# Linear attention on one Trainium2 core: one block for rows, convolution, projection and residual in place of two

## The chip, the cores and the metric

The kernel runs on one core of a Trainium2 chip. It is one program: two decoder layers over 2048 rows of 256 features, float32 outside, with a cross attention to 1601 context rows in each layer. The metric is the device time of the whole program in microseconds. The engines are TensorE (PE, with PEld for its weight loads), VectorE (DVE), ScalarE (ACT), GpSimd (POOL) and SyncE (SP); each works through its own queue in order, and they wait for one another through semaphores.

## What the part in question computes

The second layer's self attention is a linear attention with a short convolution over rows. Cut to what matters:

```python
q = _norm_last(_norm_last(jax.nn.relu(q) + EPS) ** 3)      # k the same
kv = jnp.einsum('bhnd,bhne->bhde', k, v)
z = 1.0 / (jnp.einsum('bhnd,bhd->bhn', q, k.sum(axis=2)) + EPS)
out = jnp.einsum('bhnd,bhde,bhn->bhne', q, kv, z)
xp = jnp.pad(out, ((0, 0), (1, 1), (0, 0)))
conv = xp[:, 0:N] * w_dwc[:, 0] + xp[:, 1:N + 1] * w_dwc[:, 1] + xp[:, 2:N + 2] * w_dwc[:, 2] + b_dwc
x = x + (out + conv) @ w_proj.T + b_proj
```

Each row of `out + conv` needs the row before and the row behind it, so a tile of 128 rows needs one row of each neighbour tile.

## The kernel before

There are T = 16 tiles of 128 rows. `focused_qkv` leaves the normalised q rows in `qf` (the profile calls the tensor q_rows) and the accumulated k-by-v product in the PSUM tensor `ps_kv`. Then the stage in question has two blocks with a barrier of all engines between them.

**Block one, `linear_attention`.** VectorE first builds `bd`, the block-diagonal k-by-v matrix with 8 more columns for the denominators. Then per tile n, with two buffers of each kind: GpSimd copies the q rows to `qs` (L1505); TensorE transposes them (`turn_q`, L1514); ScalarE evicts them to `qt` (`turned`, L1558); TensorE multiplies by `bd` into `ps_n` (L1530); VectorE adds the epsilon to the denominators (L1595), takes the reciprocal (L1597) and scales the numerators into `o` (L1600); TensorE transposes `o` (`turn_o`, L1521); ScalarE evicts it to `ot`, which has features on partitions and rows on the free axis (L1551), and evicts it two more times, once per half of the features, into `yt` with the middle tap and the tap bias (L1553). After the last tile VectorE adds the left and the right tap for all 2048 rows in four instructions of 2048 elements per partition (L1610).

**Block two, `linear`, called with `direct`.** ScalarE copies a tile of `yt` to `xt` (L221), TensorE projects it with four matmul records per tile (L199), VectorE adds the product to `x` (L297) and takes the row statistics with bn_stats (L299). Beside it GpSimd adds the projection's bias to `x` (L306). VectorE's add waits for that.

Behind both comes `layer_norm()`, which needs the statistics of all tiles, and then `one_head_setup`. Names in the profile: lqs, lqt, lpsq, lpsn, lpso, lo, lz, lrz, lot are the tensors of block one, conv_out is `yt`, x_res is `x`, stats is `st`.

## Time and profile before

| what | us |
|---|---|
| time, median of 3 runs (range) | 1981.6 (1980.54 to 1982.35) |
| time of the profiled execution | 1982.44 |
| its span | 1980.7 |
| VectorE's first instruction of block one starts | 1630.61 |
| VectorE's last bn_stats of block two ends (1688.97 + 0.43) | 1689.40 |

The span is the time between the first and the last recorded instruction; the profiled execution took 1.74 us more than its span. The two last lines are times from the start of the span. A timeline row has the start, the duration, the engine, the line of the kernel, the operation with output and inputs, how many instructions were merged into it, and in brackets how long the engine had been idle and who released it.

### The profile page before, as it was taken

How to read it: one execution, taken by the hardware profiler on the slowest of the kernel's cores; microseconds unless marked ns; L12 is line 12 of the kernel's file. 1: busy time of each engine (PE TensorE's matmuls, PEld its weight loads, DVE VectorE, ACT ScalarE, POOL GpSimd, SP SyncE). 2: the span in 40 equal slices, each digit the busy share in tenths (PEclk: the TensorE clock that was granted, in tenths of full speed). 3: DMA queues.
4: the chain of work that ended last, by engine and by line, in shares of the span. 5: the costliest groups of instructions: out<-in, count | busy, mean ns of one | idle time of the engine just before them, and what ended most of it. 6: DMA issues, size and time to landing. Idle time of an engine off the chain costs nothing. (4 is left out here: it accounts for less than half of the span.)

```text
span 1980.7 us, 39829 instructions
## 1 busy us (share of the span) xinstructions
PE 1725.5 (87%) x15104; PEld 694.0 (35%) x15104; DVE 1611.1 (81%) x2278; ACT 1357.1 (69%) x2607; POOL 334.5 (17%) x605
## 2 busy tenths in 40 slices
PE   7757989999999999998999999999889766499972
PEld 3421222332332233233222222222444344266651
DVE  3789999989989998887999999996578686666647
ACT  3324979889889988987999999999533445244432
POOL 0810001111121111002101010100245233000004
PEclk9966999999999999999999999999999898799995
DMA  4000000000000000100000000000300000000001
GB/s 125 0 0 1 2 1 1 2 1 1 2 1 2 1 1 1 52 1 1 2 1 2 2 1 2 1 1 2 110 1 1 1 0 1 0 1 1 1 2 42
DMA packets 12687, 18.59 MB, mean 9 GB/s; under 512 B 1856, under 2 KB 10560, under 8 KB 12256
## 3 DMA queue, kind: packets, MB, share of 16 engines
q1 hardware_dynamic: 11664, 14.78, 2.3%
q8 instruction: 121, 1.98, 0.4%
q10 hardware_dynamic: 848, 1.38, 0.2%
q14 instruction: 54, 0.44, 0.1%
HBM read 14.07 MB, written 2.10 MB: 8 GB/s over the span
## 5 line engine op out<-in xcount | busy, mean ns | idle before, releaser
L985 DVE TENSOR_REDUCE mxp<-ps_m 128x2 f32<-128x1024 f32 (+1 forms) x960 | 1088.6, 1187 | 93.7 <-PE ps_m L788 92.6
L920 ACT ACTIVATE work<-ps_s 128x512 f32<-128x512 f32 x1856 | 1010.7, 598 | 135.2 <-PE ps_s L801 87.4
L815 PE MATMUL ps_av<-work,vst 128*32 128x256 f32 x7424 | 596.8, 393 | 11.9 <-ACT avs L927 11.3
L788 PE MATMUL ps_m<-k_stack,qa 48*128 48x512 f16 (+1 forms) x2048 | 380.0, 369 | 24.1 <-DVE mxp L985 23.5
L801 PE MATMUL ps_s<-qb,k_stack 50*128 50x512 f16 x1856 | 365.9, 384 | 30.7 <-ACT work L920 24.9
L815 PEld LDWEIGHTS ps_av<-work,vst 128*32 128x32 f32 x7424 | 147.4, 108 | 347.6 <-ACT work L920 259.1
L801 PEld LDWEIGHTS ps_s<-qb,k_stack 50*128 50x128 f16 x1856 | 109.5, 93 | 424.3 <-ACT work L920 407.8
L788 PEld LDWEIGHTS ps_m<-k_stack,qa 48*128 48x128 f16 x2048 | 105.6, 95 | 66.4 <-DVE mxp L985 56.1
L646 POOL TENSOR_SCALAR mtmp<-negm 128x16 f32<-128x16 f32 x32 | 8.2, 257 | 530.9 <-DVE negm L990 530.8
L199 PE MATMUL prod<-w_qkv,xt 128*128 128x512 f32 (+1 forms) x256 | 91.9, 502 | 6.7 <-DVE k_rows L1134 6.4
L1968 DVE TENSOR_TENSOR opl<-ops_p,oph 128x512 f16<-128x512 f32 x64 | 36.3, 588 | 42.6 <-ACT oph L1892 42.5
L900 ACT COPY qb<-ps_s 128x1024 f16<-128x1024 f16 x32 | 32.6, 1018 | 48.3 <-PE ps_s L740 48.3
L199 PEld LDWEIGHTS prod<-w_qkv,xt 128*128 128x128 f32 x256 | 47.1, 194 | 44.7 <-issue 35.2
L1892 ACT CAST oph<-ops_p 128x512 f16<-128x512 f32 x64 | 30.9, 507 | 39.9 <-PE ops_p L1808 39.9
L1818 PE MATMUL ops_o<-rows_h,oph 128*128 128x192 f16 (+1 forms) x208 | 51.2, 246 | 0.6 <-DVE x_res L1982 0.6
L1820 PE MATMUL ops_o<-rows_h,opl 128*128 128x192 f16 (+1 forms) x208 | 51.1, 246 | 0.0
L1819 PE MATMUL ops_o<-rows_l,oph 128*128 128x192 f16 (+1 forms) x208 | 51.1, 246 | 0.0
L632 POOL COPY vst<-v_rows 128x1024 f32<-128x1024 f32 (+1 forms) x32 | 30.6, 957 | 120.7 <-PE ps_av L815 120.6
L601 POOL CAST qnat<-q_rows 128x256 f16<-128x256 f32 x60 | 22.3, 400 | 160.5 <-issue 86.3
L1235 PE MATMUL mprodp<-k_stack,mxh 128*128 128x512 f16 x128 | 49.0, 383 | 0.0
L1234 PE MATMUL mprodp<-k_stack,mxh 128*128 128x512 f16 x128 | 49.0, 383 | 0.0
L740 PE MATMUL ps_s<-identh,qnat 128*128 128x128 f16 x512 | 41.3, 226 | 8.4 <-DVE qnat L603 4.7
(346 smaller groups left out, 2002.5 us busy)
## 6 DMA issues: line engine op xcount, KB each, us to landing
x_res<-in_x SPq DMA_DIRECT2D x4, 512.0 KB, 14.1
w_experts<-in_w_experts SPq DMA_DIRECT2D x1, 2048.0 KB, 7.8
out<-x_res SPq DMA_DIRECT2D x8, 256.0 KB, 2.1
ctx_c<-in_ctx_c SPq DMA_DIRECT2D x1, 1664.0 KB, 8.2
ctx_n<-in_ctx_n SPq DMA_DIRECT2D x1, 1248.0 KB, 11.5
work<-in_ctx_t SPq DMA_DIRECT2D x1, 784.0 KB, 11.7
w_qkv<-in_w_qkv ACTq DMA_DIRECT2D x1, 768.0 KB, 11.5
w_qkv<-in_w_qkv SPq DMA_DIRECT2D x1, 768.0 KB, 4.2
```

Source lines behind the costliest of these rows:

```text
L199: m = pe.matmul(prod[p][:, b, 0:hi - lo], xt[p][0:rows, k, :], w[0:rows, k, lo:hi], start=(k == 0), stop=(k == 1))
L740: m = pe.transpose(out[:, j * QC + a, :], qnat[n % 2][:, a, 2 * j:2 * j + 2, :], identh[:, :])
L788: m = pe.matmul(ps_m[:, b, e, col:col + width], qa[n % 3][e * HALF:e * HALF + MAXROWS, j, a, :], STACKS[g][e * HALF:e * HALF + MAXROWS, gr ...
L801: pe.matmul(ps_s[:, banks[e], :], STACKS[part(n)][rows, pair, keys], qb[n % 2][rows, j, :, :], start=True, stop=True).then_inc(s["sc"], 1)
L815: m = pe.matmul(ps_av[32 * h:32 * h + 32, cols], vst[n % 2][:, t, h, :], pbuf[(tau[n] + t) % 2][:, h, cols], start=(t == 0 and half == 0), ...
L920: a.activation(pbuf[g % 2][:, h, :], ps_s[:, b, :], ACT.Exp, scale=factor).then_inc(s["exp"], 1)
L985: v.tensor_reduce(dst, src, AX.X, ALU.max).then_inc(s["mred"], 1)
L1234: pe.matmul(prod[:, b, :], xh[n % 2][:, k, :], weh[:, k, cols], start=(k == 0), stop=False)
L1235: pe.matmul(prod[:, b, :], xh[n % 2][:, k, :], wel[:, k, cols], start=False, stop=False)
L1818: pe.matmul(att, ph[0:r, t, :], vh[0:r, t, :], start=(t == 0), stop=False)
L1819: pe.matmul(att, ph[0:r, t, :], vl[0:r, t, :], start=False, stop=False)
L1820: m = pe.matmul(att, pl[0:r, t, :], vh[0:r, t, :], start=False, stop=(t == TM - 1))
```

## The change

The two blocks become one, and all its loops are written out. There is a list of steps n = 0 to 21, and in each step every engine does its part for a few tiles:

- GpSimd no longer copies the q rows: TensorE transposes straight from `qf`. GpSimd instead adds the projection's bias to `x` tile by tile, and adds the left tap (`left`): a two-input addition of 512 elements per partition, or 256 in the last two windows.
- ScalarE adds the epsilon to the denominators on their way out of PSUM (`denominator`), which VectorE did before. It evicts a transposed tile once (`out`) and no more twice over for the middle tap. The middle tap is instead done from SBUF for a window of tiles at once (`middle`), together with the product for the left tap, into a tensor `lt`.
- The tiles are in WINDOWS of 4, 4, 4, 2 and 2. In step hi, where a window ends, and in the step behind it, ScalarE does `middle` for one half of the features each; in step hi + 2 VectorE adds the right tap (`right`) for both halves.
- The projection of tile k is issued by TensorE in step DUE[k], straight from `yt` (`project`), into the PSUM tensor `ps_kv`, which is free once `bd` is made. VectorE adds it to `x` and takes the statistics in the step behind.
- The reciprocal's operands z and rz have two buffers each.

The diff, with most of the removed lines (which stand in the functions above) left out:

```diff
--- before.py
+++ after.py
@@ -1467,118 +1467,167 @@
                second=second, side_end=lambda act: squares(act, T - 1, (T - 1) % UNROLL))
-def linear_attention(prog, qf, ps_kv, yt, tap, tap_bias, mask, ident):
+def linear_attention(prog, x, st, qf, ps_kv, tap, tap_bias, w, bias, mask, ident):
     nc = prog["nc"]
...
+    s = {k: fresh(prog, "la_" + k) for k in ("set", "pad", "tq", "qt", "num", "z", "rz", "o", "to", "ot", "mid", "left", "conv",
+                                             "prod", "bias", "x", "st")}
     PH = P // HD
     N = P + PH
+    WINDOWS = [(0, 4), (4, 8), (8, 12), (12, 14), (14, 16)]
+    DUE = [7, 8, 9, 10, 11, 12, 13, 14, 15, 16, 16, 17, 17, 18, 19, 20]
+    STEPS = DUE[-1] + 2
     with ExitStack() as cx:
         def sb(name, shape):
             return cx.enter_context(nc.sbuf_tensor(name, shape, F32))
         bd, ks, tap1 = sb("lbd", [P, 2, N]), sb("lks", [P, 2]), sb("ltap1", [P, 2])
...
+        qt, o = ([sb(f"l{k}{p}", [P, 2, P]) for p in range(2)] for k in ("qt", "o"))
+        z, rz = ([sb(f"l{k}{p}", [P, 2, PH]) for p in range(2)] for k in ("z", "rz"))
+        ot, yt, lt, eps = sb("lot", [P, 2, S + 2]), sb("lyt", [P, 2, S]), sb("llt", [P, 2, 512]), sb("leps", [P, 1])
         ps_q, ps_n, ps_o = ([cx.enter_context(nc.psum_tensor(f"lps{k}{p}", [P, 2, 256], F32)) for p in range(2)] for k in "qno")
         block = cx.enter_context(nc.Block())
...
+        @block.tensor
+        def _(pe):
+            def turn_q(n):
+                if n >= 2:
+                    pe.wait_ge(s["qt"], n - 1)
+                for j in range(2):
+                    m = pe.transpose(ps_q[n % 2][:, j, 0:P], qf[:, n, j * P:j * P + P], ident[:, :])
+                m.then_inc(s["tq"], 1)
+            def numerator(n):
+                pe.wait_ge(s["qt"], n + 1)
+                if n >= 2:
+                    pe.wait_ge(s["o"], n - 1)
+                for j in range(2):
+                    m = pe.matmul(ps_n[n % 2][:, j, 0:N], qt[n % 2][:, j, :], bd[:, j, :], start=True, stop=True)
+                m.then_inc(s["num"], 1)
+            def turn_o(n):
+                pe.wait_ge(s["o"], n + 1)
+                if n >= 2:
+                    pe.wait_ge(s["ot"], n - 1)
+                for j in range(2):
+                    m = pe.transpose(ps_o[n % 2][:, j, 0:P], o[n % 2][:, j, :], ident[:, :])
+                m.then_inc(s["to"], 1)
+            def project(k):
+                for i, (lo, hi) in enumerate(WINDOWS):
+                    if k == lo:
+                        pe.wait_ge(s["conv"], 2 * i + 2)
+                if k >= 2:
+                    pe.wait_ge(s["x"], k - 1)
+                for j in range(2):
+                    m = pe.matmul(ps_kv[:, k % 2, 0:D], yt[:, j, k * P:k * P + P], w[:, j, :], start=(j == 0), stop=(j == 1))
+                m.then_inc(s["prod"], 1)
+            turn_q(0)
+            pe.wait_ge(s["set"], 6)
+            for n in range(STEPS):
+                if n + 1 < T:
+                    turn_q(n + 1)
+                if n < T:
+                    numerator(n)
+                if 1 <= n <= T:
+                    turn_o(n - 1)
+                for k in range(T):
+                    if DUE[k] == n:
+                        project(k)
+        @block.scalar
+        def _(a):
+            def turned(n):
+                a.wait_ge(s["tq"], n + 1)
+                if n >= 2:
+                    a.wait_ge(s["num"], n - 1)
+                a.copy(qt[n % 2][:, :, :], ps_q[n % 2][:, :, 0:P]).then_inc(s["qt"], 1)
+            def denominator(n):
+                a.wait_ge(s["num"], n + 1)
+                a.activation(z[n % 2][:, :, :], ps_n[n % 2][:, :, P:N], ACT.Identity, bias=eps[:, :]).then_inc(s["z"], 1)
+            def out(n):
+                a.wait_ge(s["to"], n + 1)
+                a.copy(ot[:, :, n * P + 1:n * P + P + 1], ps_o[n % 2][:, :, 0:P]).then_inc(s["ot"], 1)
+            def middle(i, lo, hi, j):
+                c0, c1 = lo * P, hi * P
+                a.wait_ge(s["ot"], hi)
+                a.activation(yt[:, j, c0:c1], ot[:, j, c0 + 1:c1 + 1], ACT.Identity, bias=tap_bias[:, j:j + 1],
+                             scale=tap1[:, j:j + 1])
+                if i > 0:
+                    a.wait_ge(s["left"], 2 * i + j - 1)
+                a.activation(lt[:, j, 0:c1 - c0], ot[:, j, c0:c1], ACT.Copy, scale=tap[:, j, 0:1]).then_inc(s["mid"], 1)
+            a.wait_ge(s["pad"], 2)
+            turned(0)
+            a.wait_ge(s["set"], 1)
+            for n in range(STEPS):
+                if n + 1 < T:
+                    turned(n + 1)
+                if n < T:
+                    denominator(n)
+                if 1 <= n <= T:
+                    out(n - 1)
+                for i, (lo, hi) in enumerate(WINDOWS):
+                    for j in range(2):
+                        if n == hi + j:
+                            middle(i, lo, hi, j)
         @block.gpsimd
         def _(g):
...
+            def biased(n):
+                g.tensor_tensor(x[:, n, :], x[:, n, :], bias[:, :], ALU.add).then_inc(s["bias"], 1)
+            def left(i, lo, hi):
                 for j in range(2):
...
+                    g.wait_ge(s["mid"], 2 * i + j + 1)
+                    g.tensor_tensor(yt[:, j, lo * P:hi * P], yt[:, j, lo * P:hi * P], lt[:, j, 0:(hi - lo) * P], ALU.add)\
+                     .then_inc(s["left"], 1)
+            for n in range(8):
+                biased(n)
+            for i, (lo, hi) in enumerate(WINDOWS):
+                left(i, lo, hi)
+                if i < 2:
+                    for n in range(8 + 4 * i, 12 + 4 * i):
+                        biased(n)
         @block.vector
         def _(v):
+            def shares(n):
+                p = n % 2
+                v.wait_ge(s["z"], n + 1)
+                v.reciprocal(rz[p][:, :, :], z[p][:, :, :]).then_inc(s["rz"], 1)
+                v.wait_ge(s["rz"], n + 1)
+                if n >= 2:
+                    v.wait_ge(s["to"], n - 1)
+                v.tensor_tensor(o[p][:, :, :].rearrange("p j (h d) -> p j h d", d=HD),
+                                ps_n[p][:, :, 0:P].rearrange("p j (h d) -> p j h d", d=HD),
+                                rz[p][:, :, :].unsqueeze(3).to_broadcast([P, 2, PH, HD]), ALU.mult).then_inc(s["o"], 1)
+            def right(i, lo, hi):
+                v.wait_ge(s["ot"], min(hi + 1, T))
+                for j in range(2):
+                    c0, c1 = lo * P, hi * P
+                    v.wait_ge(s["left"], 2 * i + j + 1)
+                    v.scalar_tensor_tensor(yt[:, j, c0:c1], ot[:, j, c0 + 2:c1 + 2], tap[:, j, 2:3], yt[:, j, c0:c1],
+                                           ALU.mult, ALU.add).then_inc(s["conv"], 1)
+            def add(k):
+                v.wait_ge(s["prod"], k + 1)
+                v.wait_ge(s["bias"], k + 1)
+                v.tensor_tensor(x[:, k, :], ps_kv[:, k % 2, 0:D], x[:, k, :], ALU.add).then_inc(s["x"], 1)
+            def statistics(k):
+                v.wait_ge(s["x"], k + 1)
+                v.bn_stats(st[:, k, :], x[:, k, :]).then_inc(s["st"], 1)
+            v.memset(eps[:, :], EPS_FOCUS).then_inc(s["pad"], 1)
+            v.memset(ot[:, :, 0:S + 2:S + 1], 0.0).then_inc(s["pad"], 1)
             c = Counted(v, s["set"])
...
             c(v.tensor_scalar(tap1[:, :], tap[:, :, 1], 1.0, None, ALU.add))
             c(v.tensor_copy(ks[:, :], ps_kv[:, :, P]))
             for j in range(2):
@@ -1586,30 +1635,17 @@
             v.wait_ge(s["set"], 2)
             for j in range(2):
                 c(v.tensor_scalar(bd[:, j, P:N], mask[:, 0:P:HD], ks[:, j:j + 1], None, ALU.mult))
...
+            for n in range(STEPS):
+                if n < T:
+                    shares(n)
+                for k in range(T):
+                    if DUE[k] + 1 == n:
+                        add(k)
+                        statistics(k)
+                for i, (lo, hi) in enumerate(WINDOWS):
+                    if n == hi + 2:
+                        right(i, lo, hi)
+            v.wait_ge(s["st"], T)
 def steps_of(v, c, src, mg):
@@ -2318,14 +2354,9 @@
         recycle(prog)
         end_load(prog, (s_layer1, 16 * len(layer1_in)))
         layer_norm()
-        with ExitStack() as cx:
-            yt = sb(cx, "conv_out", [P, 2, S])
-            with ExitStack() as cy:
-                ps_kv = cy.enter_context(nc.psum_tensor("ps_kv", [P, 2, 512], F32))
-                focused_qkv(prog, x, mean, rstd, w1, qn, ps_kv, ident)
-                linear_attention(prog, qn, ps_kv, yt, tap, tap_bias, mask, ident)
-            add, early = biased_residual(prog, x, st, b1p)
-            linear(prog, T, None, w1p, D, add, 2, direct=lambda n: yt[:, :, at(n * P, P)], early=early)
+        with nc.psum_tensor("ps_kv", [P, 2, 512], F32) as ps_kv:
+            focused_qkv(prog, x, mean, rstd, w1, qn, ps_kv, ident)
+            linear_attention(prog, x, st, qn, ps_kv, tap, tap_bias, w1p, b1p, mask, ident)
         layer_norm()
         with ExitStack() as cx:
             vh, vl = sb(cx, "rows_h", [P, TM, C], F16), sb(cx, "rows_l", [P, TM, C], F16)
```

On **TensorE** in the middle of the block, the queue before has three pieces of work per tile: the transposition of q, the numerators with their denominators, the transposition of o.

```order
L1514 MATMUL lpsq<-ident,lqs 128x128 x2
L1530 MATMUL lpsn<-lbd,lqt 128x136 x2
L1521 MATMUL lpso<-ident,lo 128x128 x2
L1514 MATMUL lpsq<-ident,lqs 128x128 x2
L1530 MATMUL lpsn<-lbd,lqt 128x136 x2
```

Now, from step 7 on, a projection stands behind each of these triples (lyt is the convolved tensor, ps_kv the product).

```order
L1497 MATMUL lpsq<-ident,q_rows 128x128 x2
L1505 MATMUL lpsn<-lbd,lqt 128x136 x2
L1513 MATMUL lpso<-ident,lo 128x128 x2
L1523 MATMUL ps_kv<-w_proj,lyt 128x256 x2
L1497 MATMUL lpsq<-ident,q_rows 128x128 x2
L1505 MATMUL lpsn<-lbd,lqt 128x136 x2
L1513 MATMUL lpso<-ident,lo 128x128 x2
L1523 MATMUL ps_kv<-w_proj,lyt 128x256 x2
```

What moved: 9 of the 16 projections stand between the tiles' work, and the last 7 behind it.

On **ScalarE** near the first window, the queue before repeats one pattern for each tile (lqt is the transposed q, lot the transposed output, conv_out the middle tap).

```order
L1558 COPY lqt<-lpsq 128x256
L1551 COPY lot<-lpso 128x2x128
L1553 ACTIVATE conv_out<-lpso,tap_bias,ltap 128x128 x2
L1558 COPY lqt<-lpsq 128x256
L1551 COPY lot<-lpso 128x2x128
L1553 ACTIVATE conv_out<-lpso,tap_bias,ltap 128x128 x2
```

Now, in steps 3 to 6 (lz is the denominators, llt the product for the left tap):

```order
L1545 COPY lqt<-lpsq 128x256
L1549 ACTIVATE lz<-lpsn,leps 128x16
L1553 COPY lot<-lpso 128x2x128
L1558 ACTIVATE lyt<-lot,tap_bias,ltap 128x512
L1562 ACTIVATE llt<-lot,taps 128x512
L1545 COPY lqt<-lpsq 128x256
L1549 ACTIVATE lz<-lpsn,leps 128x16
L1553 COPY lot<-lpso 128x2x128
L1558 ACTIVATE lyt<-lot,tap_bias,ltap 128x512
L1562 ACTIVATE llt<-lot,taps 128x512
L1545 COPY lqt<-lpsq 128x256
L1549 ACTIVATE lz<-lpsn,leps 128x16
```

What moved: the two short activations of every tile are gone, and two long ones stand in two consecutive steps per window, ahead of the next tile's q and denominators.

On **VectorE** from step 7 on, the queue now has the addition to x and its statistics between the tiles' work, and the right tap behind some of them; before, all rows from L1610 on stood behind the last tile.

```order
L1603 RECIPROCAL lrz<-lz 128x16
L1607 TENSOR_TENSOR lo<-lpsn,lrz 128x256
L1622 TENSOR_TENSOR x_res<-ps_kv,x_res 128x256
L1626 BN_STATS stats<-x_res 128x6
L1616 SCALAR_TENSOR_TENSOR lyt<-lot,taps,lyt 128x512 x2
L1603 RECIPROCAL lrz<-lz 128x16
L1607 TENSOR_TENSOR lo<-lpsn,lrz 128x256
```

This is step 10 with the head of step 11: the second window's right tap stands ahead of the next tile's reciprocal.

## Rows read from the trace of the kernel before

**Rows 1.** The page: granted TensorE clock in 40 slices of the span, in tenths.

```profile
PEclk9966999999999999999999999999999898799995
```

**Rows 2.** Windows of the stage; after each engine its busy us, then PEclk.

```profile
1630.50:1635.00 4.50, 3.52 (x14) 2.92 (x14) 1.94 (x10) 1.11 (x3) 2.60 (x7) 0.50 0.00 0
...
1635.00:1655.00 20.00, 17.88 (x115) 13.43 (x114) 12.77 (x45) 18.98 (x59) 3.62 (x9) 0.99 0.01 1
...
1665.80:1689.50 23.70, 19.05 (x64) 12.01 (x64) 13.63 (x32) 6.34 (x16) 10.96 (x16) 0.92 0.00 0
```

**Rows 3.** Timeline, start of the block: start us, us, engine, line, operation.

```profile
1630.61 0.06 DVE L1581 MEMSET lot<- 128x4 f32 x1 [3.09 <-PEq L158]
...
1632.60 1.27 PE L1530 MATMUL lpsn<-lbd,lqt 128*128 128x136 f32 x4
...
1635.66 0.63 PE L1530 MATMUL lpsn<-lbd,lqt 128*128 128x136 f32 x4
```

**Rows 4.** Timeline, one tile of the steady stretch, three engines.

```profile
1650.03 0.73 PE L1530 MATMUL lpsn<-lbd,lqt 128*128 128x136 f32 x4
...
1650.60 0.38 PE L1521 MATMUL lpso<-ident,lo 128*128 128x128 f32 x2
...
1650.81 0.38 PE L1514 MATMUL lpsq<-ident,lqs 128*128 128x128 f32 x2
...
1650.82 0.41 ACT L1558 COPY lqt<-lpsq 128x256 f32<-128x256 f32 x1
...
1651.01 0.25 DVE L1597 RECIPROCAL lrz<-lz 128x16 f32<-128x16 f32 x1
...
1651.07 0.43 ACT L1551 COPY lot<-lpso 128x256 f32<-128x256 f32 x1
...
1651.27 0.73 PE L1530 MATMUL lpsn<-lbd,lqt 128*128 128x136 f32 x4
...
1651.29 0.42 DVE L1600 TENSOR_TENSOR lo<-lpsn,lrz 128x256 f32<-128x256 f32 x1
...
1651.33 0.87 ACT L1553 ACTIVATE conv_out<-lpso,tap_bias,ltap 128x128 f32<-128x128 f32 x2
...
1652.03 0.44 ACT L1558 COPY lqt<-lpsq 128x256 f32<-128x256 f32 x1
```

**Rows 5.** Timeline, from the block to linear.

```profile
1655.86 9.26 DVE L1610 SCALAR_TENSOR_TENSOR conv_out<-lot,taps,conv_out 128x2048 f32<-128x2048 f32 x4 [1.65 <-ACT conv_out L1553]
...
1666.32 4.50 PE L199 MATMUL prod<-w_proj,xt 128*128 128x256 f32 x12 [11.61 <-ACT xt L221]
```

**Rows 6.** Timeline, the end of linear.

```profile
1685.09 3.33 PE L199 MATMUL prod<-w_proj,xt 128*128 128x256 f32 x12 [0.19 <-DVE stats L299]
...
1688.51 0.42 DVE L297 TENSOR_TENSOR x_res<-prod,x_res 128x256 f32<-128x256 f32 x1 [0.18 <-PE prod L199]
1688.97 0.43 DVE L299 BATCH_NORM_STATS2 stats<-x_res 128x6 f32<-128x256 f32 x1
```

**Rows 7.** Single lines: count, then duration in ns min/median/max, first and last start.

```profile
L1553 ACT ACTIVATE conv_out<-lpso,tap_bias,ltap x32: 458/468/556, 1635.9 to 1655.4; 128x128 f32<-128x128 f32 x16, 128x128 f32 x16
...
L1402 ACT ACTIVATE fa<-fb,feps x16: 733/734/736, 1559.3 to 1620.2; 128x512 f32<-128x512 f32 x16
...
L2136 POOL TENSOR_TENSOR fyq<-fy,fmagic x8: 1262/1264/1265, 1944.3 to 1972.1; 128x512 bf16<-128x512 f32 x8
...
L306 POOL TENSOR_TENSOR x_res<-x_res,b_proj x16: 722/728/737, 1665.8 to 1676.1; 128x256 f32 x12, 128x256 f32<-128x256 f32 x4
...
L1425 DVE TENSOR_TENSOR fcube<-fsquare,fa x16: 677/684/692, 1564.7 to 1625.7; 128x512 f32<-128x512 f32 x16
```

**Rows 8.** VectorE and GpSimd at once in focused_qkv: timeline, and the line.

```profile
1615.48 0.62 POOL L1439 TENSOR_TENSOR fk<-fcube,frs 128x256 f32<-128x256 f32 x1
...
1615.70 0.95 DVE L1417 TENSOR_TENSOR fa<-fa,frs 128x512 f32<-128x512 f32 x1
...
L1417 DVE TENSOR_TENSOR fa<-fa,frs x16: 691/692/949, 1561.3 to 1623.2; 128x512 f32<-128x512 f32 x16
```

More of the change, by code:

```diff
@@ L1482, in linear_attention @@
         bd, ks, tap1 = sb("lbd", [P, 2, N]), sb("lks", [P, 2]), sb("ltap1", [P, 2])
-        qs, qt = [sb(f"lqs{r}", [P, D]) for r in range(UNROLL)], [sb(f"lqt{p}", [P, 2, P]) for p in range(2)]
-        z, rz, o = sb("lz", [P, 2, PH]), sb("lrz", [P, 2, PH]), [sb(f"lo{p}", [P, 2, P]) for p in range(2)]
-        ot = sb("lot", [P, 2, S + 2])
+        qt, o = ([sb(f"l{k}{p}", [P, 2, P]) for p in range(2)] for k in ("qt", "o"))
+        z, rz = ([sb(f"l{k}{p}", [P, 2, PH]) for p in range(2)] for k in ("z", "rz"))
@@ L1486, in linear_attention @@
+        ot, yt, lt, eps = sb("lot", [P, 2, S + 2]), sb("lyt", [P, 2, S]), sb("llt", [P, 2, 512]), sb("leps", [P, 1])
         ps_q, ps_n, ps_o = ([cx.enter_context(nc.psum_tensor(f"lps{k}{p}", [P, 2, 256], F32)) for p in range(2)] for k in "qno")
         block = cx.enter_context(nc.Block())
-        def every(body, eng):
-            with eng.Fori(0, T // UNROLL - 1) as i:
-                for r in range(UNROLL):
-                    body(UNROLL * i + r, r)
-            for n in range(T - UNROLL, T):
-                body(n, n % UNROLL)
@@ L1496, in has @@
-        def has(n):
-            return not (type(n) is int and n >= T)
+        @block.tensor
[41 more added lines that the diff above has]
+                        project(k)
@@ L1546, in _ @@
-        @block.scalar
-        def _(a):
-            def out(n, p):
-                a.wait_ge(s["to"], n + 1)
-                a.copy(ot[:, :, at(n * P + 1, P)], ps_o[p][:, :, 0:P]).then_inc(s["ot"].sem, 1)
-                for j in range(2):
-                    a.activation(yt[:, j, at(n * P, P)], ps_o[p][:, j, 0:P], ACT.Identity, bias=tap_bias[:, j:j + 1],
-                                 scale=tap1[:, j:j + 1]).then_inc(s["ot"].sem, 1)
-            def turned(n, p):
-                s["tq"].wait(a, n + 1)
-                a.copy(qt[p][:, :, :], ps_q[p][:, :, 0:P]).then_inc(s["qt"].sem, 1)
-            s["qt"].open(a)
-            s["ot"].open(a)
-            a.wait_ge(s["set"], 6)
-            def body(n, r):
-                if has(n + 1):
-                    turned(n + 1, 1 - r % 2)
-                if not (type(n) is int and n == 0):
-                    out(n - 1, 1 - r % 2)
-            turned(0, 0)
-            for n in range(UNROLL):
-                body(n, n)
-            with a.Fori(1, T // UNROLL - 1) as i:
-                for r in range(UNROLL):
-                    body(UNROLL * i + r, r)
-            for n in range(T - UNROLL, T):
-                body(n, n % UNROLL)
-            out(T - 1, 1)
@@ L1580, in _ @@
+            def statistics(k):
[3 more added lines that the diff above has]
+            v.memset(ot[:, :, 0:S + 2:S + 1], 0.0).then_inc(s["pad"], 1)
             c = Counted(v, s["set"])
-            v.memset(ot[:, :, 0:S + 2:S + 1], 0.0).then_inc(s["conv"], 1)
             c(v.tensor_scalar(tap1[:, :], tap[:, :, 1], 1.0, None, ALU.add))
```

65 lines of the change are left out of this document (removed).

## The prediction

> **What bounds the stage now.** I read the page first, for the clock of TensorE over the span [rows 1]: it is at its upper level nearly everywhere, so nothing outside the stage hangs on it. The stage itself runs from VectorE's first instruction at 1630.61 [rows 3] to the end of the last bn_stats at 1688.97 + 0.43 = 1689.40 [rows 6], **58.8 us**. What comes before and behind is not touched. The windows by stretch [rows 2] show three regimes: 20 us in which ScalarE is busy 18.98, while VectorE is busy 12.77; then the convolution; then 23.7 us in which VectorE is busy only 13.63 and ScalarE 6.34.
>
> The timeline of one tile shows why ScalarE sets the first stretch [rows 4]: its instructions start back to back at 1650.82, 1651.07, 1651.33 and again 1652.03. A copy of 256 elements holds it 0.25 us, although its record lasts 0.41, and the two short activations hold it 0.70. The period is 1.24 us (numerators at 1650.03 and 1651.27). TensorE's own need for a tile is 0.57 (1650.03 to 1650.60) + 0.21 + about 0.22 for the other transposition = **1.0 us**. Behind the last tile the whole convolution lies bare: 9.26 us of VectorE in four instructions, and the first projection starts only at 1666.32 [rows 5]. TensorE is idle for 11.6 us there. Of the stage's time, then, the convolution and the barrier cost about 11 us and the projection about 23 us, both with nothing of the attention beside them.
>
> **The parts of the change, and their prices.** I count by steps of the new list, since the engines work in order.
>
> *Per tile on ScalarE.* Gone: 0.70 us. New: the denominators, 16 elements. Below, its price is bounded by the 0.25 that a 256-element copy holds the engine [rows 4], above by the 0.468 of a 128-element activation with bias and scale [rows 7]; I take 0.25 held and 0.30 until the result is there. New per window and half: two activations of 512. The nearest row is 0.734 for 512 elements with a bias [rows 7]. The short ones of 0.468 [rows 7] start 0.35 apart (0.70 for two), so an instruction holds the engine 0.12 less than its record says; that gives 0.61 to 0.73 each. I take 0.67, 1.35 for both. A step without a window costs ScalarE 0.75, one with a window 2.1.
>
> *On VectorE.* Gone: the epsilon instruction and its wait. Left per tile: reciprocal to scaling 0.28 and the scaling 0.42 [rows 4], 0.75 with the gap behind. Moved here: add to statistics 0.46, statistics 0.43 [rows 6], 0.93 with a gap. The right tap of 512 elements: below 2.35/4 = 0.59 from the four long ones (9.26 us for four) [rows 5], above 0.95 from the slowest two-input row of 512 [rows 8]; the common two-input row of 512 has 0.684 [rows 7]. I take 0.70, so 1.4 per large window and 0.9 per small one. All of VectorE is 16 x (0.75 + 0.93) + 3 x 1.4 + 2 x 0.9 = 33 us.
>
> *On TensorE.* Tiles 16 x 1.0. A projection: 12 records in 3.33 us at the end of linear are 1.1 us for four [rows 6]. 16 of them are 17.7. Together 33.7 us, about the same as VectorE. The block becomes a race of two equal engines, with one in-order chain through ScalarE.
>
> *On GpSimd.* The copies of q go (hidden, but for the first, which TensorE's first transposition waited for). The bias stays at 0.728 a tile. The left tap: 1.26 for 512 two-input elements [rows 7], 10 instructions, 10 us in all. 22 us in 40 is not a bound, but it lies in the chain of the first window.
>
> *Beside it.* The copy of `yt` on ScalarE and the barrier go, both counted in the 58.8. No new DMA. The 22 steps are straight code in place of loops; the tails of the old loops are straight code too, and run faster than the loop (add to statistics 0.46 in the tail).
>
> **The sum.**
>
> 1. Head. The first numerator waits for `bd`, no longer for GpSimd's copy. It started 2.0 us in (1632.60) [rows 3]; what the copy took of that lies between nothing (if `bd` was as late) and 1 us; I take 0.6, which leaves 1.4.
> 2. Steps 0 to 6. TensorE starts cold, at 0.50 [rows 2]: numerators last 1.27 instead of 0.73 [rows 3, 4]. Three steps at 1.45 = 4.35. Two at 1.05 = 2.1. In steps 4 and 5 ScalarE's first window stands ahead of the next tile's q and denominators: two at 2.05 = 4.1. Then TensorE must wait for the first window: second half of `middle` done, 1.25 for GpSimd's left tap, two right taps 1.4, together 2.65. Sum **13.2**.
> 3. Projection 0 and steps 8 to 15. TensorE needs 1.0 + 1.1 = 2.1 a step. VectorE needs 4 x 1.68 + 1.4 = 8.1 in four steps, and the waits for GpSimd (below) bring it to 8.8, 2.2 a step. 1.1 + 8 x 2.2 = **18.7**.
> 4. Tail, from the end of projection 8 to the last statistics, on VectorE: five additions with statistics (k = 8 to 12) 4.65, the two small right taps 1.8. Projection 14 waits for the last right tap: two projections 2.2 + gap 0.15 + the last add and statistics 0.9 = 3.25. Sum **9.7**.
>
> 1.4 + 13.2 + 18.7 + 9.7 = 43.0 against 58.8: **15.8 us less**. On the profiled execution 1982.44 - 15.8 = 1966.6; on the median of the runs, 0.84 lower, **1965.8**.
>
> **Where rows speak against it: VectorE and GpSimd at once.** The two-input VectorE instruction at 1615.70 took 0.95 us where its median is 0.692, and it began while GpSimd's two-input one was running (1615.48 to 1616.10) [rows 8]. In the new block each right tap reads two SBUF tensors, and GpSimd goes on with two-input work of 0.73 or 1.26 us as soon as a left tap is done. I charge 0.35 for each of the four right taps of windows 0 and 1, of which those of window 1 are in the 8.8 and window 0's hide mostly behind GpSimd's end of the second half. The Trainium skill, "SBUF — State Buffer", section "SBUF: two separate sides", says more: the shared pair of ports is a lock held for a whole instruction, so the loser is blocked fully. By that a right tap could wait a whole bias addition (0.73) and four would cost up to 2.9 us in place of 1.4; the sum would be 1967.3. The 0.95 of the row fits a lock whose holder had 0.4 left no better than a shared port, so the trace does not decide.
>
> **The rivals.**
>
> *The lists mesh fully.* What speaks for it: both bounds are 33 to 34 us, and ScalarE's total is only 16 x 0.75 + about 11 = 23. If windows cost TensorE nothing but the cold start (1.2 more) the stage is 1.4 + 33.7 + 1.2 + 0.9 = 37.2, 21.6 less: 1960.0. Against: in step 7 nothing but the first window's chain can release projection 0, and the last window has the same tail.
>
> *The in-order queues lock step.* If in every step of 8 to 15 the chain numerators, denominators, reciprocal, scaling, transposition of o (0.73 + 0.3 + 0.28 + 0.48 = 1.8) has VectorE's add and statistics in its way (0.9), a step takes 2.7 to 2.8: 8 x 0.55 = 4.4 more, 1.5 more in steps 4 to 7 and 2 in the tail. The stage is 51, 1974. Against: two buffers of each kind let the add of step n run while TensorE does the next projection (1.1).
>
> *Slower: the clock falls.* TensorE alone needs 33.7 us at the upper level (2.4 GHz). At 0.50, the lower level (1.2 GHz), it needs 67.4, and with head and end 70: 11 slower, 1993. It decides from a mean granted clock under 33.7/56.5 = 0.60. Against: the old block, with TensorE waiting 0.2 us in every tile, had 0.99, and linear, busy 19 of 23.7, had 0.92 [rows 2]; the new wait at step 7 of about 2 us is far shorter than the 11.6 behind which linear began cold. "TensorE: Matmul & The Clock Gate", part 1, in the Trainium skill says that an idle stretch throttles the array; no stretch so long is left in the new block.
>
> *Nothing moves* (a gain within 0.2%, 4 us) would need 11 us of new waits; I see no place for them but the lock step made twice as bad.
>
> **How the numbers follow.** Forecast, stage 40 to 47 us, 0.72; full mesh 0.12; lock step 0.12; nothing moves 0.02; slower 0.02. Range: steps 8 to 15 at 2.05 to 2.5 (-1.2 to +2.4), first window hidden or worse (-2 to +1.5), tail +-1, head +-0.4; together 41 (1963.5) to 48 us (1970.8). Down to 1960.5 it takes in most of the full mesh, up to 1971 the mild half of lock step. What a measurement of this kernel tells from no change is about 0.2%. Faster 0.96, same 0.02, slower 0.02.
>
> **What the profile after should show.** First numerator 1.4 us after the memset. ScalarE back to back in steps 4 and 5, TensorE waiting there and again before projection 0, with VectorE's right tap as releaser. From then TensorE steps of about 2.2 us at full clock. The last seven projections alone, the last two released by the right tap. All wrong if steps 8 to 15 take over 2.6, or if TensorE's clock reads 0.5 behind step 3. A right tap of over 1 us would show the lock.

## The result, and the profile after

The changed kernel takes **1968.59 us** (median of 4 runs, 1967.9 to 1969.09) against 1981.07 (4 runs of before beside it). The ratio is 0.9936, 95% interval 0.9919 to 0.9953. That is 12.5 us less; the forecast was 15.8 less, and the range held the time. The profiled execution has a span of 1967.3, 13.4 less than before. Of these, the stage gives 12.3: it starts at 1630.98 and ends with the last statistics at 1677.00 + 0.43 = 1677.43, **46.45 us** against 58.79 (forecast 43.0). Behind the stage the program took 289.9 instead of 291.3, and ahead of it 0.4 more; neither part was changed.

The page shows that the engines' busy time hardly moved (TensorE 1725.5 before) and that the clock has nearly the same pattern, with one slice lower by a tenth [rows 1]:

```profile
PE 1719.1 (87%) x15104; PEld 694.4 (35%) x15104; DVE 1606.1 (82%) x2269; ACT 1355.7 (69%) x2595; POOL 341.1 (17%) x599
...
PEclk9966999999999999999999999999999898699995
```

So what was saved is waiting. The windows of the stage, which answer to [rows 2]:

```profile
1630.90:1635.00 4.10, 2.55 (x11) 2.18 (x12) 2.07 (x8) 1.00 (x3) 4.06 (x6) 0.50 0.00 0
1635.00:1639.00 4.00, 4.00 (x20) 3.90 (x20) 2.03 (x6) 2.33 (x8) 1.45 (x3) 0.50 0.00 0
1639.00:1648.00 9.00, 5.50 (x38) 4.18 (x37) 4.62 (x11) 6.68 (x19) 4.29 (x4) 0.99 0.00 0
...
1648.00:1668.60 20.60, 16.24 (x100) 13.89 (x101) 15.17 (x38) 13.57 (x35) 12.58 (x13) 1.00 0.00 1
1668.60:1677.50 8.90, 6.77 (x30) 4.92 (x28) 8.13 (x21) 2.27 (x5) 1.46 (x2) 1.00 0.00 1
```

Between 1639 and 1668.6 no engine is busy more than 0.8 of the time. TensorE's clock is at its lower level, 0.50, up to 1639, 8 us into the block; before it was at 0.99 from 4.4 us on.

The head, from the timeline (answers to [rows 3]):

```profile
1630.94 5.51 POOL L1582 TENSOR_TENSOR x_res<-x_res,b_proj 128x256 f32<-128x256 f32 x8 [1.59 <-SPq L1481]
...
1631.03 0.66 DVE L1631 TENSOR_SCALAR ltap<-taps 128x2 f32<-128x2 f32 x1
...
1631.67 0.47 DVE L1634 TENSOR_TENSOR lbd<-ps_kv,head_mask 128x128 f32<-128x128 f32 x2
...
1632.07 0.99 DVE L1637 TENSOR_SCALAR lbd<-head_mask,lks 128x8 f32<-128x8 f32 x2
...
1633.59 1.11 PE L1505 MATMUL lpsn<-lbd,lqt 128*128 128x136 f32 x4
```

VectorE's set-up instructions that read only SBUF, one of 2 elements and two of 8, take 0.66 and together 0.99 us beside GpSimd's bias additions. The product with the mask, with PSUM as one input, takes 0.47 as before. The first numerator starts 2.61 us into the block.

Steps 10 and 11 of the same timeline show where TensorE waits (compare [rows 4]):

```profile
1653.98 1.27 POOL L1587 TENSOR_TENSOR lyt<-lyt,llt 128x512 f32<-128x512 f32 x1 [0.75 <-ACT llt L1562]
...
1655.01 0.41 DVE L1622 TENSOR_TENSOR x_res<-ps_kv,x_res 128x256 f32<-128x256 f32 x1
...
1655.21 3.73 POOL L1582 TENSOR_TENSOR x_res<-x_res,b_proj 128x256 f32<-128x256 f32 x4
...
1655.46 0.43 DVE L1626 BATCH_NORM_STATS2 stats<-x_res 128x6 f32<-128x256 f32 x1
...
1655.80 1.86 DVE L1616 SCALAR_TENSOR_TENSOR lyt<-lot,taps,lyt 128x512 f32<-128x512 f32 x2
1657.59 0.24 DVE L1603 RECIPROCAL lrz<-lz 128x16 f32<-128x16 f32 x1
1657.72 0.73 PEld L1523 LDWEIGHTS ps_kv<-w_proj,lyt 128*128 128x128 f32 x4 [2.38 <-DVE lyt L1616]
1657.72 1.13 PE L1523 MATMUL ps_kv<-w_proj,lyt 128*128 128x256 f32 x4 [2.14 <-DVE lyt L1616]
```

The left tap ends at 1655.25, and VectorE then still has the rest of an addition and the statistics ahead of the right taps; the two right taps take 1.86 us beside GpSimd's bias additions. Projection 4, which is next in TensorE's queue, starts after 2.14 idle us, and the next tile's work stands behind it.

Of TensorE's waits in the stage, the four for a right tap are by far the largest; two for the transposed q, behind ScalarE's window, follow (columns: us in total, times, longest):

```profile
PE ps_kv L1523 <- DVE lyt L1616: 6.6, 4, 2.1
...
PE lpsn L1505 <- ACT lqt L1545: 1.5, 2, 1.1
```

The groups by line show the prices: an eviction of the denominators 276 ns, a right tap of 512 elements 980 ns and one of 256 elements 474.

```profile
L1616 DVE SCALAR_TENSOR_TENSOR lyt<-lot,taps,lyt 128x512 f32<-128x512 f32 x6 | 5.6, 980 | 0.0
...
L1549 ACT ACTIVATE lz<-lpsn,leps 128x16 f32<-128x16 f32 x16 | 4.4, 276 | 2.4 <-PE lpsn L1505 2.0
...
L1616 DVE SCALAR_TENSOR_TENSOR lyt<-lot,taps,lyt 128x256 f32<-128x256 f32 x4 | 1.7, 474 | 0.0
```

### The profile page after: what moved, and what is told of

It is laid out like the page before. It is cut to its first block and busy times, and to the rows that moved or that the text cites. A ratio compares the mean times of both kernels' runs of the same rounds, so it can differ in the third digit from the quotient of the medians.

```text
span 1967.3 us, 39498 instructions
## 1 busy us (share of the span) xinstructions
PE 1719.1 (87%) x15104; PEld 694.4 (35%) x15104; DVE 1606.1 (82%) x2269; ACT 1355.7 (69%) x2595; POOL 341.1 (17%) x599
## 6 DMA issues: line engine op xcount, KB each, us to landing
x_res<-in_x SPq DMA_DIRECT2D x4, 512.0 KB, 14.4
```

## The experiments

In all of them the stage is measured as above, in the profiled execution; "behind" is the rest of the span after it. There is one profiled execution for each kernel, and whole executions of one kernel lie up to 4 us apart (e1: 1965.69 to 1969.73; its profiled one is the longest). How far the stage of one kernel varies was not measured. The nearest check is between kernels that differ little: e9 and e11 have 44.82 and 44.80, e12 and e13 43.64 and 43.66.

| run | edit | time, us | ratio to before (95%) | stage | behind |
|---|---|---|---|---|---|
| before | | 1981.07 | | 58.8 | 291.3 |
| after | | 1968.59 | 0.9936 (0.9919 to 0.9953) | 46.45 | 289.9 |
| e1 | bias behind the set-up | 1967.09 | 0.9929 (0.9912 to 0.9945) | 46.9 | 289.7 |
| e2 | no bias | 1970.10 | 0.9949 (0.9932 to 0.9965) | 45.7 | 294.3 |
| e3 | projections later | 1967.26 | 0.9934 (0.9917 to 0.9951) | 46.9 | 289.6 |
| e4 | projections behind all | 1973.72 | 0.9967 (0.9955 to 0.9978) | 53.7 | 289.5 |
| e5 | right tap first | 1969.61 | 0.9939 (0.9922 to 0.9956) | 45.75 | 294.4 |
| e6 | windows of two | 1967.77 | 0.9926 (0.9909 to 0.9942) | 47.0 | 289.2 |
| e8 | bias in gaps | 1968.57 | 0.9932 (0.9916 to 0.9949) | 46.2 | 290.0 |
| e9 | e8 and e5 | 1963.56 | 0.9907 (0.9891 to 0.9924) | 44.8 | 288.2 |
| e10 | idle work at the head | 1971.93 | 0.9953 (0.9936 to 0.9970) | 50.15 | 289.6 |
| e11 | e9, last bias moved | 1964.77 | 0.9921 (0.9904 to 0.9937) | 44.8 | 288.2 |
| e12 | e11, idle work in the waits | 1964.84 | 0.9921 (0.9904 to 0.9937) | 43.6 | 289.4 |
| e13 | e12, idle work at the end | 1964.19 | 0.9916 (0.9899 to 0.9933) | 43.7 | 289.1 |

The start of the block also differs between kernels, 1627.9 to 1631.4, though nothing ahead of it was edited. A difference of 2 or 3 us between two times of this table need therefore not be the stage's; the stage column is what the edits are judged by.

**e1, bias later.** Against the changed kernel:

```diff
+            g.wait_ge(s["set"], 6)
             for n in range(8):
                 biased(n)
```

> Stage = from VectorE's first instruction of the block to the end of its last statistics; 46.45 us in the changed kernel, 58.8 before. Ports theory (VectorE's SBUF-only instructions wait while GpSimd adds the bias): with GpSimd's first bias addition behind the six set-up instructions, VectorE's rows for the tap and the denominators' columns fall from 0.66 and 0.99 back to 0.17 and 0.54, the first numerator starts 0.9 us earlier, stage 45.5 or less. Queue-order theory (the later head is TensorE's second transposition standing behind the wait for the set-up): these two rows stay as they are and the stage stays at 46.4.

The two rows fell to 0.17 and 0.36, and the first numerator started 1.48 us into the block, 1.1 earlier. So it was GpSimd's additions that held VectorE up. But the stage got no shorter. The windows of this run say why:

```profile
1643.90:1646.20 2.30, 0.75 (x5) 0.31 (x3) 2.27 (x4) 0.89 (x3) 2.30 (x3) 1.00 0.00 0
1646.20:1649.40 3.20, 3.15 (x12) 2.75 (x13) 0.58 (x2) 0.43 (x2) 1.94 (x3) 0.57 0.02 5
...
1665.00:1667.10 2.10, 0.02 (x1) 0.00 (x0) 2.10 (x4) 1.40 (x5) 1.35 (x2) 1.00 0.00 0
1667.10:1670.50 3.40, 3.36 (x9) 2.71 (x10) 2.55 (x8) 0.79 (x2) 0.57 (x1) 0.50 0.00 0
```

Behind two of TensorE's waits for a right tap the granted clock was 0.57 and 0.50 for over 3 us, and the projections and numerators there ran at about half speed. In the changed kernel the same waits left it at 1.00. In this execution the clock took what the head gave; whether it fell at these two waits in the kernel's other executions is not shown. Their mean granted clock is 0.946 to 0.947, against 0.944 here, and ahead of the block this execution had the lower level for 10 us more than most other kernels.

**e2, no bias.** This kernel leaves the projection's bias out of its result.

```diff
-                g.tensor_tensor(x[:, n, :], x[:, n, :], bias[:, :], ALU.add).then_inc(s["bias"], 1)
+                g.sem_inc(s["bias"], 1)
```

> The projection's bias is left out of the result. Ports theory: besides the 0.9 us at the head, the right taps of 512 elements fall from a mean of 0.98 to about 0.70 in windows 0 and 1 (window 2 still meets a left tap), stage 43.5 to 44.5. Lock-step theory (the first projection of a window stands too early in TensorE's queue, and VectorE then waits for TensorE): only the head comes back, stage about 45.5, TensorE's waits for the right tap stay near 2 us each.

The right taps of windows 0 and 1, from the timeline (two instructions each):

```profile
1640.67 1.45 DVE L1616 SCALAR_TENSOR_TENSOR lyt<-lot,taps,lyt 128x512 f32<-128x512 f32 x2
...
1651.28 1.40 DVE L1616 SCALAR_TENSOR_TENSOR lyt<-lot,taps,lyt 128x512 f32<-128x512 f32 x2
```

They fell from 1.93 and 1.86 to 1.45 and 1.40, which is the 0.70 of the prediction for each; window 2, where GpSimd has a left tap, stayed at 1.85. The mechanism is as the ports theory says, the stage is not: 45.7 instead of 43.5 to 44.5, again with the clock at 0.61 behind the first projection and 0.67 in the tail. The whole program was no faster than the changed kernel (1970.10), with 294.3 us behind the stage.

**e3, projections later.**

```diff
-    DUE = [7, 8, 9, 10, 11, 12, 13, 14, 15, 16, 16, 17, 17, 18, 19, 20]
+    DUE = [7, 8, 9, 10, 12, 13, 14, 15, 16, 16, 17, 17, 18, 18, 19, 20]
```

> Projections 4 to 15 one step or so later than in the changed kernel, so that a window's first projection no longer stands ahead of the next tile's work. Lock-step theory: TensorE's idle time before the projections falls from 6.6 us to about 3, VectorE's wait for the denominators falls too, stage 43.5 to 45. VectorE-bound theory (four steps cost VectorE 4 x 1.68 + 1.9 = 8.6 and the rest is waiting that only moves): stage 46 to 47.

The wait moved. TensorE's idle time for the right tap fell from 6.6 us to 1.4 (in the waits from 1640 on), and 4.2 came up for the scaled numerators, which stand behind the right tap in VectorE's queue:

```profile
1655.19 0.44 PE L1513 MATMUL lpso<-ident,lo 128*128 128x128 f32 x2 [2.07 <-DVE lo L1607]
```

So it does not help by itself to move the projection in TensorE's queue: what TensorE could do instead needs VectorE too. The stage's 46.9 has one fall of the clock in it, 0.66 in the 3.3 us behind this wait, which the changed kernel had not; so a gain of up to 1 us from the later projections is not excluded, and the run does not decide between its two theories.

**e4, projections behind everything.**

```diff
-    DUE = [7, 8, 9, 10, 11, 12, 13, 14, 15, 16, 16, 17, 17, 18, 19, 20]
+    DUE = [19, 19, 19, 19, 20, 20, 20, 20, 21, 21, 21, 21, 22, 22, 23, 24]
```

> All 16 projections, with their additions and statistics, behind the last right tap (steps 19 to 24), the convolution still in windows beside the tiles. If running the projection beside the tiles is what pays: the stage goes back to 54 to 57 us. If what pays is the hidden convolution and the shorter projection part (four matmul records in 1.07 instead of 1.4 us a tile): head 2.6, 16 tiles at 1.3 to 1.4, 3 for the last window, 16 x 1.07 and 1 at the end, stage 46 to 49.

53.7, just under the first theory's 54. This splits the 12.3 us: 5.1 come without any projection beside the tiles, and 7.3 from running them there. A part of the 7.3 is clock: behind window 2's right tap the clock was at 0.50 from 1662.5 to 1666 and at 0.85 in the mean from there to the end. The third and fourth addition came 1.79 and 1.66 us behind the one before, where the later ones, at the upper level, came every 0.86; that is some 1.7 us. The timeline of TensorE from one window's first numerators to the next:

```profile
1640.57 0.73 PE L1505 MATMUL lpsn<-lbd,lqt 128*128 128x136 f32 x4 [1.06 <-ACT lqt L1545]
...
1645.98 0.44 PE L1513 MATMUL lpso<-ident,lo 128*128 128x128 f32 x2 [1.35 <-DVE lo L1607]
...
1648.60 0.73 PE L1505 MATMUL lpsn<-lbd,lqt 128*128 128x136 f32 x4 [1.06 <-ACT lqt L1545]
```

Four tiles take 8.03 us, against 4 x 1.24 = 5.0 in the old block, and even ScalarE, the busiest, is then busy only 0.8 of the time (7.96 of 10 us, the second number from the end of the busy times):

```profile
1640.00:1650.00 10.00, 6.01 (x40) 4.67 (x40) 5.05 (x12) 7.96 (x22) 7.45 (x7) 1.00 0.01 2
```

With the projections in between, the changed kernel takes 9.73 for the same four (numerators at 1649.17 and 1658.90). The projections beside the tiles cost 1.7 us in four tiles. What is dear is the windows themselves: the two middle taps on ScalarE and the right taps on VectorE stand ahead of the next tile.

**e5, right tap first.** In VectorE's steps, `right` goes ahead of `add` and `statistics`:

```diff
+                for i, (lo, hi) in enumerate(WINDOWS):
+                    if n == hi + 2:
+                        right(i, lo, hi)
                 for k in range(T):
                     if DUE[k] + 1 == n:
                         add(k)
                         statistics(k)
...
```

> In VectorE's queue the right tap of a window stands ahead of the addition and statistics of its step. Stage in the changed kernel 46.45. Order theory (0.8 us of addition and statistics stand ahead of what TensorE waits for): the left tap is done 0.55 us before the right tap now starts, so the first projection of windows 1 and 2 starts 0.5 earlier each, stage 45.0 to 45.6. VectorE-bound theory: what moves behind the tap only makes the next tile later, stage 46.2 to 46.6.

45.75, 0.7 less, and nearer to the order theory's 45.0 to 45.6 than to the other's 46.2 to 46.6. As in the changed kernel, the clock did not fall in the stage once it had risen, so this pair is not disturbed by it. The program was no faster, since this run took 4.5 us more behind the stage.

**e6, windows of two.**

```diff
+    WINDOWS = [(2 * i, 2 * i + 2) for i in range(8)]
+    DUE = [k + 5 for k in range(16)]
```

> Taps in eight windows of two tiles, projection k in step k + 5. In-order-chain theory (it is the long pieces, 1.35 us of middle taps in each of two steps and 1.9 us of right tap, that stand ahead of the next tile): pieces of half the size, TensorE's waits shrink to under 1 us each, steps of about 2.0 us throughout, stage 43 to 45. Fixed-cost theory (twice as many small instructions, ScalarE 27 us, VectorE 35 us): 46 to 48.

47.0, within the range of the fixed-cost theory and outside the other's. TensorE now waits for a right tap eight times, 9.1 us in all and up to 1.4, and two tiles take 5.01 us. But the number of instructions is not all that changed: in six of the eight windows the two right taps took 1.37 to 1.54 us, against 0.86 in the last two windows here and in the changed kernel. GpSimd's bias additions or left taps lay beside them. These 0.5 to 0.7 us a window are contention, and no run parts them from the fixed cost.

**e8, bias in gaps; e9, with the right tap first; e11, the last bias moved.**

```diff
                      .then_inc(s["left"], 1)
+                    if j == 0 and i < 4:
+                        biased(12 + i)
...
+            g.wait_ge(s["set"], 6)
+            for n in range(12):
                 biased(n)
```

This is e8. e9 adds e5's edit. e11 has `i < 3` in place of `i < 4`, and `biased(15)` behind the last left tap.

> GpSimd adds the bias to 12 tiles behind the set-up and to one tile in each gap between two left taps, so that none of it lies beside a right tap. Ports theory: head 1.5 instead of 2.6 us, the right taps of windows 0 and 1 take 1.40 instead of 1.93 and 1.86, window 2 stays at 1.85; stage 44.3, or 45.5 if TensorE's clock falls once in it, as it did in two runs. If the right taps are slow for another reason they stay at 1.9.

> The two edits before this one together. If both theories hold the gains add: 43.3 to 44.3; if VectorE is the bound, only that of the bias's place stays, 44.3 to 45.

> Right tap first and the bias placed in gaps (stage 44.82 in that run), with the last bias addition behind the last left tap instead of beside window 2's right tap. Ports theory: window 2's right tap falls from 1.99 to 1.85 or less, stage 44.5 to 44.8. It is the control of the two kernels that follow.

In e8 the right taps were 1.45, 1.40 and 2.32: as expected in windows 0 and 1, worse in 2, where a bias addition and a left tap both met it. The stage of e8 was 46.2, above the 44.3 and the 45.5 expected, with the clock down behind the first projection and again in the tail. With the right tap first (e9) it was 44.82, and 44.80 in e11. That is above the 43.3 to 44.3 at which both gains would simply add, and inside the range of "VectorE is the bound"; but it is 1.4 below e8, which that theory does not give either. The clock fell twice in each of these three runs and not once in e5, and still e9 is 0.9 shorter than e5: the placing of the bias pays. Window 2's tap was at 1.99 in e9 and stayed there in e11, where 1.85 or less was expected: in these two it is the next window's left tap that it meets, not the bias. e9 has the lowest time of all, 1963.56; its interval reaches from 0.9891 to 0.9924, that of the changed kernel from 0.9919 up, so the two overlap.

**e10, idle work at the head.**

```diff
             turn_q(0)
+            for _ in range(6):
+                pe.transpose(ps_q[1][:, 1, 128:256], ident[:, :], ident[:, :])
             pe.wait_ge(s["set"], 6)
```

> The changed kernel with six idle transpositions on TensorE while it waits for the set-up at the head; nothing else moves. Clock theory (the slow head kept TensorE idle, and so its clock rose only 7.8 us into the block, against 4.4 before): the numerators reach 0.63 us a record by step 2 or 3 instead of step 4, the first projection starts 1 to 1.5 us earlier against the block's start, stage about 45.2. If the clock does not depend on it: stage 46.4.

The first half came: the numerators were at 0.63 from step 2, and the first projection started 1.3 us earlier against the block's start. The second half is the clearest miss of the study, 50.15 instead of 45.2. The windows around the waits:

```profile
1646.40:1649.70 3.30, 3.30 (x11) 2.82 (x12) 0.49 (x2) 0.37 (x1) 1.85 (x3) 0.50 0.00 0
...
1656.00:1658.70 2.70, 0.69 (x7) 0.45 (x6) 2.67 (x6) 0.96 (x3) 2.70 (x4) 1.00 0.00 0
1658.70:1662.00 3.30, 3.30 (x13) 2.96 (x14) 1.40 (x5) 0.65 (x2) 1.20 (x2) 0.59 0.00 0
...
1667.00:1669.70 2.70, 0.57 (x6) 0.26 (x4) 2.67 (x6) 1.95 (x6) 1.65 (x3) 0.97 0.00 0
1669.70:1673.00 3.30, 3.30 (x9) 2.66 (x10) 2.44 (x7) 0.73 (x2) 0.53 (x1) 0.51 0.00 0
```

and the places that answer to the last four in the changed kernel:

```profile
1655.00:1657.70 2.70, 0.58 (x5) 0.26 (x3) 2.67 (x6) 0.86 (x3) 2.70 (x4) 1.00 0.00 0
1657.70:1661.00 3.30, 3.28 (x21) 2.98 (x22) 2.36 (x8) 1.77 (x5) 1.24 (x2) 1.00 0.00 0
1664.70:1667.40 2.70, 0.52 (x3) 0.20 (x2) 2.67 (x6) 2.00 (x6) 1.64 (x3) 1.00 0.00 0
1667.40:1670.70 3.30, 3.08 (x14) 2.37 (x14) 3.20 (x9) 1.84 (x5) 0.96 (x2) 1.00 0.01 2
```

TensorE is as busy in the 2.7 us ahead (0.69 and 0.57 us against 0.58 and 0.52), but in e10 the clock is at about the lower level for the 3.3 us behind and fewer instructions are done: 13 and 9 against 21 and 14. A third fall, behind the wait for window 0, was the longest: the clock was at 0.50 up to 1649.7 and at 0.78 in the mean from there to 1656. So the clock did depend on the idle work at the head, but not to the stage's gain.

**e12 and e13, idle work in the waits and at the end.** Against e11:

```diff
                     if k == lo:
+                        for _ in range((10, 8, 14, 0, 8)[i]):
+                            pe.transpose(ps_q[DUE[k] % 2][:, 0, 0:P], ident[:, :], ident[:, :])
                         pe.wait_ge(s["conv"], 2 * i + 2)
```

That is e12. e13 adds 12 more such transpositions behind the last projection.

> As the control, with 10, 8, 14 and 8 idle transpositions on TensorE ahead of its wait for the right tap of windows 0, 1, 2 and 4. Clock theory (a wait of about 2 us for a right tap lets the granted clock fall to 0.5 for the 3.3 us behind it, which costs 1 to 1.6 us each time): the clock stays at 1.0 from step 4 on, stage 43.0 to 43.6. If the slow records behind the waits have another cause: 44.5 or more, since the idle transpositions only take time.

> As the kernel before, with 12 more idle transpositions behind the last projection. The time from the end of the stage to the end of the program was 289.9 us in the changed kernel but 294.4 in the one with the tap first, whose clock was at 0.5 to 0.57 for the first 10 us behind the stage. If the clock at the stage's end decides that: 288 to 290 here. If not, 294 can come here too.

The stage fell from 44.80 to 43.64 and 43.66, at the upper edge of what the clock theory had. In e12 the clock never went down again once it had risen:

```profile
1642.10:1645.40 3.30, 3.30 (x23) 2.96 (x22) 1.60 (x6) 1.74 (x5) 0.00 (x0) 1.00 0.00 0
1645.40:1661.90 16.50, 15.54 (x104) 13.24 (x103) 13.16 (x33) 11.83 (x32) 7.92 (x8) 1.00 0.00 1
1661.90:1671.60 9.70, 7.71 (x37) 5.82 (x36) 8.52 (x21) 2.27 (x5) 2.14 (x3) 1.00 0.00 1
```

The clock of the control had fallen twice in the stage, so 1.16 us for two falls is what the idle work brings, in one trace of each. Over whole runs the 1.2 us don't show (1964.84 and 1964.19 against 1964.77). e13 had 289.1 behind the stage, but e11 had 288.2 without the idle work at the end, so it says nothing on what made 294 in e2 and e5.

## Why the prediction was right, and where it was off

**Kind and place of the gain: right.** The bare convolution and the projection with nothing beside it are gone, and e4 shows both parts (5.1 and 7.3 us, the second with some clock in it). None of the rivals came in full. Something like the lock step came once in each window, around the right tap, and not in every step. The clock rival was right in kind, though not in size: with the projections beside the tiles a fall lasted some 3.5 us (once 7, in e10) and not the whole block; but in e1, e2, e3 and e8 to e11 waits of 0.9 to 2.6 us were enough for one, where the prediction held about 2 us to be too short. e4 had one as well.

**Where the numbers met by luck.** The stage gave 12.3 us and not 15.8, because terms 1 to 3 were each 1.2 to 2 us too small and term 4 was 0.9 too large. The program came 2.8 us above the forecast and not 3.5, mainly since 1.4 us more were saved behind the stage, where the prediction had nothing. (In its range, a stage of 41 us gives 1963.8, not 1963.5; nothing hangs on it.)

**Term 1, head: 1.4 forecast, 2.61 measured.** The step that failed is that nothing but the copy of q was weighed. GpSimd's bias additions, which start at once in the new block, held up VectorE's set-up by 1.1 us (shown by e1, 1.48). The prediction had looked for that contention only at the right taps.

**Term 2, steps 0 to 6 with the wait for window 0: 13.2 forecast, 14.4 measured.** ScalarE's two long steps came as described (numerators at 1641.07, 1643.19 and 1645.22, 2.1 and 2.0 apart) and so did the wait for projection 0 (2.76 from the last of these, as the sum counts it, where 2.65 was forecast; 3.08 from the end of `middle` at 1644.90). Most of the rest is the cold clock, which lasted into step 3, a step that was forecast at the upper level; with TensorE kept busy at the head (e10) the same part took 13.13. Some 0.3 us are not clock: at the upper level step 4 took 1.33 instead of 1.05.

**Term 3, steps 8 to 15: 18.7 forecast, 20.65 measured** (from projection 0 at 1647.98 to the start of projection 9 at 1668.63). An ordinary step took 1.76 to 1.93, less than the 2.1, for the 1.1 of a projection came from a row in which projections stand back to back; between other work one holds TensorE 0.87 (1649.85 to 1650.72). A window's step took 4.27. "VectorE needs 8.1 in four steps, and the waits for GpSimd bring it to 8.8" added up work, while the chain around a right tap was not filled, and this is the step that failed: TensorE waits 2.1 us for the tap, and then VectorE up to 0.8 for TensorE's next tile (1.6 behind window 0's). Four steps took 9.73 instead of 8.8. e3 supports the chain, since the wait changed its name when the projections moved, but with a fall of the clock in it. e5 shows that a part of it is the order in VectorE's queue: with the right tap first the stage is 0.7 shorter.

**Term 4, tail: 9.7 forecast, 8.8 measured.** Additions with statistics came every 0.79 to 0.86 instead of 0.93, and the stretch from the start of the last two projections to the end took 2.92 instead of 3.25.

**The contention: right, and smaller than charged.** 0.35 for each of four right taps was charged; without GpSimd's additions two taps took 1.40 to 1.45 instead of 1.86 to 1.93, 0.24 each. For the whole lock, the Trainium skill, "SBUF — State Buffer", section "SBUF: two separate sides", says that a GpSimd instruction and a VectorE one in a two-port mode, or with two SBUF inputs while GpSimd's reads SBUF, exclude one another for a whole instruction. The head's rows agree: the SBUF-only set-up instruction that starts 0.09 behind GpSimd's first addition ends 0.75 behind its start (5.51/8 = 0.69 for one), and the one with a PSUM input is not slowed. The right taps agree too, by the sign that the prediction named, a tap of over 1 us. Single lines of both engines (ns, least, median, most), and the first bias addition beside window 0's right taps:

```profile
L1616 DVE SCALAR_TENSOR_TENSOR lyt<-lot,taps,lyt x10: 468/737/1212, 1646.0 to 1674.0; 128x512 f32<-128x512 f32 x6, 128x256 f32<-128x256 f32 x4
...
L1582 POOL TENSOR_TENSOR x_res<-x_res,b_proj x16: 722/726/1224, 1630.9 to 1658.2; 128x256 f32<-128x256 f32 x16
...
1646.20 1.18 POOL L1582 TENSOR_TENSOR x_res<-x_res,b_proj 128x256 f32<-128x256 f32 x1
```

A tap takes up to 1.21 us instead of 0.70, and a bias addition beside it up to 1.22 instead of 0.73. Beside window 0's taps the two engines' instructions end in turn, at 1646.80 (tap), 1647.38 (addition), 1647.93 (tap) and 1648.52 (addition), 0.55 to 0.59 apart, as if only one ran at a time. So the loss is shared: GpSimd's four additions there take 3.69 us instead of 2.76.

**Behind the stage.** The prediction said that nothing outside the stage hangs on the clock. The traces speak against it. Late in the next stage, from 1915 to 1919 before, the clock was at 0.57, and at the same place after it was at 1.00; from the last large activation of that stage to the layer norm behind it took 15.6 us before and 14.5 after, 1.1 of the 1.4. And over the fourteen traces the length of the part behind the stage goes with the time for which the clock was at its lower level in it: 82.4 to 82.5 us in e9 and e11 (288.2), 85.6 to 86.0 in the changed kernel, e1, e3, e4, e6, e10, e12 and e13 (289.1 to 289.9), 89.1 in e8 (290.0), 89.3 before (291.3), 96.3 and 96.5 in e2 and e5 (294.3 and 294.4). That is about 0.44 us for each us at the lower level. It is not a tested cause, since no run sets the clock there alone, and the change did not aim at it: by what the prediction knew, the 1.4 us are luck.

## What to carry to other kernels

Before merging stages into one list of steps, draw the chain through the in-order queues for the one step that carries the long piece, and not the mean load of the engines: here the bounds were 33 and 34 us and the stage takes 46. Then move the item on which the other engine waits: the right tap ahead in VectorE's queue gave 0.7 us (e5) and 1.4 (e9 against e8), while later projections in TensorE's queue mainly renamed the wait (e3). Put GpSimd's SBUF work where VectorE does not read SBUF for something urgent, and above all not beside the set-up at the head of a block. And judge an edit of 1 us by the stage in the trace together with its clock, since the clock can return 1 to 4 us with the opposite sign; better by more than one trace, which was not done here.
